# Attention phase of a vision tower: ten products that nothing reads, ahead of the first score products of each unit

## The reference

```
h = tokenize(x)                          # 16x16 patches, norm, product 768 -> 192, norm: 64 x 196 tokens of 192
h = h + attention(norm(h))               # 12 heads of 16, softmax over 196 keys, projection
h = h + ffn_block(norm(h))               # a second attention of the same size, an MLP 192-768-192,
                                         # then 4 experts, each token to its best 2
```

## Time and profile before

| | us |
|---|---|
| median of three runs | 3173.27 |
| lowest and highest | 3169.94, 3174.86 |
| the profiled execution's own time | 3171.36 |
| its span, first to last instruction | 3169.6 |
| busy: TensorE products / weight loads | 2756.1 / 2128.4 |
| busy: VectorE, ScalarE, GpSimd | 2320.9, 1878.0, 1671.7 |
| mean granted clock of TensorE over the span | 0.947 |

### The profile page before, as it was taken

The page is one execution under the profiler, slowest core; times in us unless marked ns, Lnnn a source line. Parts: engine busy times, 40 slices in busy tenths (PEclk is TensorE's granted clock), DMA queues, the critical chain, the costliest instruction groups (busy, mean ns, idle before and its releaser), DMA issues. The chain is left out here.

```text
span 3169.6 us, 95506 instructions
## 1 busy us (share of the span) xinstructions
PE 2756.1 (87%) x31491; PEld 2128.4 (67%) x31491; DVE 2320.9 (73%) x5326; ACT 1878.0 (59%) x3798; POOL 1671.7 (53%) x1957
## 2 busy tenths in 40 slices
PE   4999379998999988989998858988984999999998
PEld 3888345555555555555555538888874888888887
DVE  4888477887878787878787726766655777777776
ACT  3888256676666666666666637666642444444443
POOL 2777325455554666666666441556554444444444
PEclk8999688999999999999999969999986999999999
DMA  5564245667666666677767635444433444444443
GB/s 140 162 188 125 58 111 136 157 151 161 147 153 151 157 165 160 159 170 163 162 162 164 152 81 139 135 128 132 129 107 95 67 67 67 68 67 67 67 67 50
DMA packets 515433, 395.07 MB, mean 125 GB/s; under 512 B 223136, under 2 KB 488386, under 8 KB 515138
## 3 DMA queue, kind: packets, MB, share of 16 engines
q1 hardware_dynamic: 431426, 310.47, 40.2%
q0 software_dynamic: 38496, 46.38, 8.3%
q10 hardware_dynamic: 45216, 34.34, 4.6%
HBM read 232.59 MB, written 155.42 MB: 122 GB/s over the span
## 5 line engine op out<-in xcount | busy, mean ns | idle before, releaser
L701 DVE TENSOR_REDUCE a_mx<-a_mxp 98x4 f32<-98x784 f32 x768 | 747.5, 973 | 278.5 <-PE a_mxp L850 275.3
L540 ACT ACTIVATE a_pt<-a_st 98x784 f32<-98x784 f32 x768 | 633.9, 825 | 364.9 <-PE a_st L836 363.8
L1609 POOL DMA_INDIRECT out_dram<-f_yo,f_idg x202 | 329.8, 1633 | 417.2 <-DVE f_yo L1950 380.7
L481 POOL TENSOR_TENSOR a_cf<-a_ctxs,a_rec 128x1176 f32<-128x1176 f32 x64 | 171.5, 2680 | 456.1 <-DMA a_rec<-a_recip 456.1
L1687 ACT ACTIVATE f_hf<-f_bank,f_b1c 128x256 f32<-128x256 f32 x606 | 253.9, 472 | 236.5 <-PE f_bank L924 236.3
L865 PE MATMUL a_pv<-a_pt,a_vp 98*32 98x196 f32 x6144 | 359.6, 353 | 5.4 <-issue 4.4
L836 PE MATMUL a_st<-a_qst,a_kst 49*128 49x196 f16 x3072 | 268.1, 254 | 78.8 <-DMA a_qst<-a_mrow 54.2
L2112 PE MATMUL f_bank<-f_w2h,f_hh 128*128 x1212 | 298.9, 247 | 14.4 <-DVE f_hl L1934 13.0
L2113 PE MATMUL f_bank<-f_w2h,f_hl 128*128 x1212 | 298.2, 246 | 0.0
L2114 PE MATMUL f_bank<-f_w2l,f_hh 128*128 x1212 | 298.2, 246 | 0.0
L850 PE MATMUL a_mxp<-a_kst,a_qst 48*128 48x196 f16 x3072 | 264.9, 251 | 27.5 <-DVE a_mx L701 22.7
(11 more groups left out here) (324 smaller groups left out, 8367.6 us busy)
## 6 DMA issues: line engine op xcount, KB each, us to landing
a_rec<-a_recip SPq DMA_DIRECT2D x256, 147.0 KB, 4.9
t_rows<-in_x_dram SPq DMA_DIRECT2D x84, 392.0 KB, 5.9
a_qst<-a_qk SPq DMA_DIRECT2D x256, 110.2 KB, 3.1
a_kst<-a_qk SPq DMA_DIRECT2D x256, 110.2 KB, 3.8
f_xg<-f_listed SPq DMA_DIRECT2D x101, 264.0 KB
a_qk<-a_qkh SPq DMA_DIRECT2D x128, 196.0 KB, 3.1
a_qk<-a_qkl SPq DMA_DIRECT2D x128, 98.0 KB, 3.4
a_qk<-a_qkh SPq DMA_DIRECT2D x128, 98.0 KB, 2.5
```

Source lines behind the costliest of these rows:

```text
L540: act.activation(pt[k % PT][:].rearrange("p j a t -> p j (a t)"), st_ps[0:half_t, :, 0:unit_t], ACT.Exp, scale=sm_scale).then_inc(exp_s, 1)
L701: dve.tensor_reduce(mx[:, a, :, 2 * p:2 * p + 2].rearrange("p q j -> p j q"), mx_ps[0:half_t, :, 0:unit_t].rearrange("p j (q t) -> p j q t ...
L1609: pool.indirect_dma_start(out, bass.IndirectOffsetOnAxis(ap=idg[i % 3][:, t:t + 1], axis=0), yo[i % 3][:, t, :], None, compute_op=ALU.add) ...
```

## The change

In slot 0 of every step that has a unit with role "C", TensorE does ten products ahead of `scores`. All ten multiply the same 128 x 128 block of weights with 256 columns of the same weights (half-precision operands) and write columns 256 to 511 of `pv_ps`, which nothing reads. They wait for nothing that isn't there already.

```
@@ -806,6 +806,8 @@
                     if k in ROWS_AT[0:2] and "L" in kinds:
                         m = ROWS_AT.index(k)
                         rows(take(f"QK{m}"), s + 3, (par + 1) % 2, m, kinds["L"])
+                    if k == 0 and "C" in kinds:
+                        keep_busy(10)
                     if "C" in kinds:
                         scores(s, par, k)
                     if k == 0 and "C" in kinds:
@@ -823,6 +825,11 @@
                         turn_maxima(s, 1)
                     if k == MAXIMA_AT[1] and "M" in kinds:
                         turn_maxima(s + 1, 0)
+
+            def keep_busy(n):
+
+                for _ in range(n):
+                    pe.matmul(pv_ps[:, 256:512], wh[0][:, 0, 0:128], wh[0][:, 0, 0:256], start=True, stop=True)
```

## The result

The changed kernel took 3192.6 us in the median of seven executions (3184.09 to 3216.6), the kernel before 3173.27 (3164.59 to 3178.23): ratio 1.0063, 95% interval 1.0037 to 1.0088, about 20 us. Two more groups of runs gave 1.0103 (1.0067 to 1.0140) and 1.0091 (1.0056 to 1.0126), about 30 us. Averaged by their intervals, the three groups give a ratio of 1.008, about 25 us, give or take 6. The forecast was 3179, with a range of 3164 to 3190, so 3192.6 lies outside it. The sign was forecast, the size was not: the cost is three to four and a half times the 6.7 us of the sum.

The account below looks back on a forecast made before the run. TensorE was taken to set the attention phase's pace, its largest wait being slot 0's for the maxima's DMA. Excess +13.5 less 6.8 by the clock gave +6.7 us, so 3179 us, range 3164 to 3190.

Parts of the forecast that it names:

- The wait bounds slot 0, and work there is hidden up to it: Slot 0: scores wait 54.2 us for the maxima's DMA; a wait of 0.91 us or more hides a block wholly.
- Size of one block, 1.08 us: Slot 0: ten products at 0.108 us each take 1.08 us at the full clock, weight loads hidden.
- The excess stays: Block time beyond slot 0's waits moves all later work along: 11.0 + 3.0 - 0.5 = 13.5 us.
- rival 1: Given back: later waits or earlier transfers take about half the excess, so no change, 3171 to 3174; chance 0.22.
- The clock, 6.8 us to gain: Three clock falls behind slot 0's longest waits go as the block fills them, saving 6.8 us together.
- the seven others: Clock falls from slots 1 to 3, expected to stay near seven, about 2.5 us each; no gain counted.
- Rival 3: More falls: the moved work meets four more low-clock stretches, +10 us, so 3189; chance 0.08.
- ±5 for the seven falls: Slots 1 to 3: moved work may hit five or nine low stretches instead of seven, about 2.5 us each.
- The unit mean that I named as a sign, 22.6: Mean unit time between 471.42 and 1821.08 us, 22.49 before, was to become about 22.6.
- A rule that speaks for more: The block in slot 0 may keep the clock up for the whole unit: second rival, 3162, chance 0.12.

Follow-up runs that it names:

- e9: The kernel before once more, no edit, for a second trace; ratio 0.9993 (0.9969 to 1.0018).
- e1: The changed kernel again, no edit; 3197.19 us against 3167.03 of the kernel before, ratio 1.0103.
- e10: The changed kernel a third time, no edit; 3149.45 us against 3118.96 of the kernel before, ratio 1.0091.
- e7: The changed kernel with the negation of the maxima on ScalarE instead of VectorE; ratio 1.0025 to the kernel before.
- e13: The kernel before with ten products in slot 0 and five in slot 2; 3127.06 us against 3121.63, ratio 1.0013.
- e3: The changed kernel with twenty products in slot 0 instead of ten; 3296.87 us, ratio 1.0389 to the kernel before.
- e5: The kernel before, no products added, with the negation of the maxima on ScalarE instead of VectorE; ratio 1.0010.

## Why the prediction was wrong

*The wait bounds slot 0, and work there is hidden up to it:* right. 54.2 us of waiting went to 4.9.

*Size of one block, 1.08 us:* the products took 0.108 each as read from the earlier trace rows, but the term was too small. Behind the last product scores come 0.10 later than its share of the engine ends, with or without a wait. It could be read before, in a unit that doesn't wait (timeline of PE, kernel before):

```profile
450.29 0.25 PE L924 MATMUL a_misc<-a_wl,a_xl 128*128 128x192 f16 x1
450.47 0.34 PE L836 MATMUL a_st<-a_qst,a_kst 49*128 49x196 f16 x4
```

0.18 from start to start, of which 0.08 is the product. I had counted this 0.10 as room. With a need of 1.18 the same 61 waits give 15.1 us instead of 11.0, and with the three units that don't wait 18.3 instead of 14.0. The traces have 0.22 to 0.31 a unit in slot 11 to 0, some 16 us.

*The excess stays:* right for ten products. A unit without a low stretch grew by 0.23 us on average, the slot by 0.27; the difference is no larger than that between two traces of one kernel, so rival 1 is out. It isn't right without limit: with twenty a fifth was given back. I had named 6.3 us of POOL's `a_cn` as the only wait that could do so, and passed over the 11.6 us of `a_xo`, which shrank to 1.0 there, when I listed the waits.

*The clock, 6.8 us to gain:* this is the step that failed. The three falls right behind long waits of slot 0 are gone, as forecast: of 25 falls in the changed kernel none begins within 2 us of scores 0. But I took the seven others as a number that stays. One of them lies in unit 61, outside my table; of the six in it, e9 has four, and the changed kernel had 5, 4 and 16. Its mean clock over all executions is 0.950 in the group of e1 and 0.949 in that of e10, where before had 0.952 and 0.9535. Only the second difference is clear of the spread by itself; the two together are 0.003, give or take 0.002. So on average the changed kernel spends more time at 1.2 GHz, not less. A mean clock lower by 0.003 over 3160 us is some 19 us more at half the clock, which cost some 9 us at the price of e10's falls (half of a low stretch): an estimate of +9 in place of -6.8. With the 16 of excess it gives 25, which is what the three groups have on average.

In the group of the result itself falls beyond those of before aren't needed: 3173.27 and an excess of 18.3 are 3191.6 (3189 with the 16 us of the traces), against 3192.6. There the gain by the clock that didn't come and the 0.10 us of each block can be the whole miss. The groups of e1 and e10 cost more than the excess. Rival 3, which I gave 0.08, is thus nearest to what happened, in its mechanism; that its 3189 lies near the result is in part luck, as its sum had the excess too small by 4 us and the gain of 6.8 still in it.

Where I read this from was also at fault: one execution. The two profiled ones differ by 12.7 us, the medians by 20 to 30, and falls of one kernel vary between 4 and 16 from trace to trace. My ±5 for the seven falls was too narrow by far. The unit mean that I named as a sign, 22.6, can't be told from such traces either: 22.51 and 22.45 in two of the changed kernel, 23.16 in e10, and 22.49 and 22.26 before. And I placed the wait for VectorE in slot 1; counted by scores, it is in slot 2.

*Why more falls with the block?* Shown is this: with twenty products in slot 0 the negations that GpSimd holds up rise from 20 to 50 of 128 and the falls from 9 to 29, and with the negation moved away there are 5. Every one of the 34 later falls in the five traces of the two kernels follows a long wait for VectorE in slot 2, and such a wait follows a held-up negation. With ten the numbers are 20, 13 and 27 held-up negations for 5, 4 and 16 falls, against 20 and 12 for 9 and 6 before; they go together, but three traces don't show that ten products make them more frequent, and e7 with none held up has 12 falls. For ten products the mechanism is therefore only partly settled. That the cost beyond the excess is falls of the clock behind slot 2 is shown for twenty products and for the trace of e10; for the ten on average it rests on the mean clocks and on e13.

*A rule that speaks for more:* I took the advice of the Trainium skill ("TensorE: Matmul & The Clock Gate", section "HAM oscillation — how this bites in real kernels") to keep the engine working for a reason why the block might hold the clock for the whole unit. In slot 0 neither ten nor twenty products did (mean clocks 0.950 and 0.938 in one group, before 0.952). In slot 2 the traces agree with it: with five or three products the clock was up (0.958 against 0.9535 and 0.953). The place decides, and it isn't that of the longest wait.

## What to carry to other kernels

A wait that is long on average is no room for work of its average length: take each wait by itself, add the hand-over to the need, and count the overrun. Here it stayed whole at 0.27 us a unit, and four fifths of it stayed at 1.2; look for waits later in the loop that can absorb some. If idle time costs through the clock, look for the wait that stands ahead of the falls and put filling work there, not where the single wait is longest, and keep it short: three products did what five did. One trace can't carry a claim on the clock; look at several executions.

## What was unexpected of the hardware

VectorE's negation, 98 x 24 elements, takes 0.17 us alone and up to 2.4 (e10) when it starts during one of GpSimd's tensor operations. Those over 0.9 us end with that operation, in all 20 cases of before, 50 of e3 and 27 of e10 within 0.12 us (666.72 + 1.64 = 668.36 against 666.18 + 2.15 = 668.33). The same work on ScalarE takes 0.21 to 0.22 us always (e5). The Trainium skill has this in "SBUF — State Buffer", section "Who interferes with whom": VectorE and GpSimd share one pair of ports under an exclusive lock, `tensor_scalar` can be in a mode that needs it, the later one waits for the whole instruction, and ScalarE waits for nobody. For this instruction the traces agree with the last two points; the ports, the lock and the mode can't be seen in them. VectorE's maxima (L701) kept their 0.97 us beside the same operations of GpSimd.

Once down, the clock mostly stayed down for 3.4 to 10.2 us, though TensorE was busy all of that time (6.80 of 6.80 us in the rows of e10). A fall made its unit 3.35 us longer in e10.
